# Sixteen-head attention: another order for VectorE, and a rounding copy handed from VectorE to GpSimd

## What is computed

```
mod = silu(c) @ W_mod + b_mod
sh, sc, g, ... = split(mod, 6)
h = layernorm(x) * (1 + sc) + sh
q, k, v = split(h @ W_qkv, 3)            # 16 heads of width 64
attn = softmax((q @ k.T) * 64 ** -0.5)   # per batch and head, 256 x 256
out = (attn @ v).reshape(B, T, 1024)
x = x + g * (out @ W_out + b_out)
```

## Time and profile before

| | before |
|---|---|
| time, median of 3 runs | 1752.8 us (1749.63 to 1753.22) |
| the profiled execution: span from the first to the last instruction | 1752.5 us |
| PE busy | 1626.4 us, 93% of the span |
| PEld busy | 1458.4 us, 83% |
| DVE busy | 1294.3 us, 74% |
| ACT busy | 1179.8 us, 67% |
| POOL busy | 1093.6 us, 62% |
| mean granted clock of TensorE, as a share of full speed | 0.978 |
| the chain that ended last, by engine | PE 64%, DVE 13%, issue 8%, POOL 6%, ACT 2% |

### The profile page before, as it was taken

One profiled execution on the slowest core, in us unless ns is written; L12 is line 12 of the kernel. 1 busy time (PEld: TensorE's weight loads), 2 busy tenths in 40 slices (PEclk: granted clock), 3 DMA queues, 4 the chain that ended last, 5 costly groups with the idle time before them and its releaser, 6 DMA issues.

```text
span 1752.5 us, 37390 instructions
## 1 busy us (share of the span) xinstructions
PE 1626.4 (93%) x13251; PEld 1458.4 (83%) x13251; DVE 1294.3 (74%) x2766; ACT 1179.8 (67%) x2896; POOL 1093.6 (62%) x1261
## 2 busy tenths in 40 slices
PE   4888998999999999999999789999999999989997
PEld 2557878888888888888888779999888889989997
DVE  3767768989898888888888745556788778864442
ACT  2545657777787777787777655556676667666663
POOL 1555667888888888888888622333555568842223
PEclk7999999999999999999999899999999999999999
DMA  8213310000000000000000011111122112221111
GB/s 306 61 49 86 88 42 11 11 10 11 11 7 6 11 10 11 11 11 11 10 11 10 1 32 30 31 31 32 48 57 58 45 27 46 47 52 37 37 49 48
DMA packets 110973, 65.93 MB, mean 38 GB/s; under 512 B 81530, under 2 KB 92788, under 8 KB 110788
## 3 DMA queue, kind: packets, MB, share of 16 engines
q1 hardware_dynamic: 110788, 63.54, 13.3%
HBM read 59.06 MB, written 4.46 MB: 36 GB/s over the span
## 4 chain that ended last, share of the span: by engine, by line
PE 64%; DVE 13%; issue 8%; POOL 6%; ACT 2%; DMA 0%; DVEq 0%; POOLq 0%; SPq 0%; ACTq 0%
PE bank L289 14%; PE bank L290 13%; PE bank L291 13%; POOL prob L1083 5%; PE s_banks L289 4%; PE bank L1105 4%; DVE ptlo L1120 4%; PE s_banks L290 4%; PE s_banks L291 4%; PE s_banks L1028 4%; PE bank L1131 3%; DVE of L1157 2%; PE bank L417 2%; DVE xn L376 2%; DVE oThi L1161 1%
## 5 line engine op out<-in xcount | busy, mean ns | idle before, releaser
L1083 POOL TENSOR_SCALAR prob<-prob,rinv 128x256 f32<-128x256 f32 x508 | 465.8, 935 | 117.0 <-DVE rinv L1064 117.0
L1055 ACT ACTIVATE prob<-s_banks,nmax 128x256 f32<-128x256 f32 x512 | 236.6, 475 | 17.4 <-DVE nmax L1045 17.4
L289 PE MATMUL bank<-WBhi,hl 128*128 128x256 f32 x768 | 219.0, 285 | 6.2 <-DVE upd L647 5.3
L290 PE MATMUL bank<-WBlo,hh 128*128 128x256 f32 x768 | 217.7, 283 | 0.0
L291 PE MATMUL bank<-WBhi,hh 128*128 128x256 f32 x768 | 215.5, 281 | 0.0
L1115 ACT ACTIVATE pthi<-bank 128x512 fp32r<-128x512 f32 x256 | 139.2, 596 | 100.9 <-PE bank L1105 98.8
L1045 DVE TENSOR_REDUCE nmax<-s_banks 128x4 f32<-128x1024 f32 x128 | 156.0, 1219 | 62.6 <-issue 61.9
L610 ACT ACTIVATE hh<-bank,vecs 128x512 fp32r<-128x512 f32 x120 | 82.9, 691 | 155.7 <-PE bank L291 155.7
L430 ACT ACTIVATE nThi<-bank,mod 128x256 fp32r<-128x256 f32 x192 | 110.5, 575 | 104.9 <-issue 75.7
L289 PE MATMUL bank<-aThi,WAlo 128*128 128x256 f32 x576 | 175.4, 304 | 0.6 <-DVE aTlo L438 0.2
L1120 DVE TENSOR_TENSOR ptlo<-bank,pthi 128x512 fp32r<-128x512 f32 x256 | 164.9, 686 | 4.0
(11 more groups left out here) (185 smaller groups left out, 5546.5 us busy)
## 6 DMA issues: line engine op xcount, KB each, us to landing
gates<-gate_scratch SPq DMA_DIRECT2D x96, 256.0 KB, 3.6
agate<-gate_scratch SPq DMA_DIRECT2D x32, 256.0 KB, 3.6
stage<-in_L_cond_W SPq DMA_DIRECT2D x64, 64.0 KB, 2.3
out<-x SPq DMA_DIRECT2D x16, 256.0 KB, 2.2
adaw<-in_L_cond_Wc SPq DMA_DIRECT2D x1, 3072.0 KB, 17.7
stage<-in_L_cond_W_qkv SPq DMA_DIRECT2D x8, 384.0 KB, 3.4
x<-in_x SPq DMA_DIRECT2D x1, 2560.0 KB, 16.6
stage<-in_L_cond_ff_w SPq DMA_DIRECT2D x32, 64.0 KB, 2.2
```

The source lines that it names most:

```text
L289: pe.matmul(dst, lhs[1], rhs[0], start=start, stop=False, skip_group_check=True)
L290: pe.matmul(dst, lhs[0], rhs[1], start=False, stop=False, skip_group_check=True)
L1055: last = act.activation(prob[h % 4][:, q, :], SB_[h % 2][:, q * SEQ:(q + 1) * SEQ], ACT.Exp, bias=of_head(nmax, h)[:, q:q + 1], accum_out= ...
L1083: last = pool.tensor_scalar(prob[h % 4][:, q, :], prob[h % 4][:, q, :], of_head(rinv, h)[:, q:q + 1], None, ALU.mult)
```

## The change

The copy of `of` to `oThi` leaves `o_add` and DVE and becomes the first instruction of `o_rest` on POOL, with the two waits that stood before it; POOL then waits for its own copy before it subtracts. In DVE's list, `o_add(n - 2)` comes ahead of `score_max(n + 2)`; statistics and normalisation come ahead of `proj_vector`; and 1/sum is made for pair n + 2 near the end of period n, ahead of the projections, where it was made for pair n + 1 at the start of period n. The first 1/sum of pair 1 moves to the end of `mh_start`.

```
-        def o_add(dve, pair, i):
+        def o_add(dve, pair):
             if pair:
                 dve.wait_ge(o_lo, pair)
...
                 dve.tensor_tensor(of[main, :], OB[main, cols], oc[main, :], ALU.add).then_inc(o_sum, 1)
-            dve.wait_ge(o_sum, 2 * pair + 2)
+
+        def o_rest(pool, pair, i):
+
+            pool.wait_ge(o_sum, 2 * pair + 2)
             if pair >= 2:
-                dve.wait_ge(out_mm, pair - 1)
-            dve.tensor_copy(oT[i][0][:, :], of[:, :]).then_inc(o_hi, 1)
-
-        def o_rest(pool, pair, i):
-
+                pool.wait_ge(out_mm, pair - 1)
+            pool.tensor_copy(oT[i][0][:, :], of[:, :]).then_inc(o_hi, 1)
             pool.wait_ge(o_hi, pair + 1)
             pool.tensor_tensor(oT[i][1][:, :], of[:, :], oT[i][0][:, :].bitcast(F32),
                                ALU.subtract).then_inc(o_lo, 1)
...
         def mh_vector(dve, b, j):
             n = PAIRS * b + j
-            if n + 1 < PERIODS:
-                prob_inverse(dve, n + 1)
             if j == 3 and b:
                 res_vector(dve, A, b - 1, YB, out_mm, PAIRS * b, b - 1)
+            if n >= 2:
+                o_add(dve, n - 2)
             if n + 2 < PERIODS:
                 score_max(dve, n + 2)
-            if n >= 2:
-                o_add(dve, n - 2, n % 2)
             for h in range(2):
                 pt_rest(dve, 2 * n + h)
             if j == NEXT - 1 and b + 1 < BATCH:
                 rows_vector(dve, b + 1)
-            for it in items(b, j):
-                proj_vector(dve, *it)
             if b + 1 < BATCH:
                 if j == 1:
                     ln_stats(dve, A, b + 1, 0)
                 if j == 2:
                     ln_norm(dve, A, b + 1, 0)
+            if n + 2 < PERIODS:
+                prob_inverse(dve, n + 2)
+            for it in items(b, j):
+                proj_vector(dve, *it)
             if j == NEXT:
                 weights_hi(dve, A + 1, b)
...
+            if name == "vector":
+                prob_inverse(eng, 1)
```

More of the change, by code:

```diff
@@ L1334, in mh_vector @@
             if n == PERIODS - 1:
-                o_add(dve, n - 1, (n - 1) % 2)
-                o_add(dve, n, n % 2)
+                o_add(dve, n - 1)
+                o_add(dve, n)
                 res_vector(dve, A, b, YB, out_mm, PAIRS * b + PAIRS, b)
```

## The result

The changed kernel takes 1768.87 us (median of 4 runs, 1766.43 to 1769.55); the kernel before, run beside it, 1751.89 us (4 runs, 1749.63 to 1753.22). The ratio is 1.01, with a 95% interval from 1.0088 to 1.0112: slower by 1.0%, where 0.7% was forecast. The profiled execution of the changed kernel has a span of 1767.8 us.

What follows compares the result with a forecast made beforehand. Four engines were nearly full together, so the order of handing work on was taken as the bound. Span 1752.5 plus 10.5 - 0.6 + 2 gives 1764.4, plus 0.3 gives 1764.7 us, 0.7% slower; range 1744 to 1779.

Steps and rivals of the forecast that it cites:

- The chain: Attention periods: exponentials, projection's high part, `o_read`, sums, maximum, exponentials close a ring; 5.47 us with one projection, 47.26 a batch.
- the two weight copies in j = 4: DVE, j = 4 to 5: they follow the projection's low part and add 0.47 us to a 5.67 us period.
- the steps: Period lengths summed over a batch: 47.26 us against 46.56, 0.70 more, so 10.5 us over 15 batches.
- not 0.6: First batch: 0.6 us less than the others, because it has no gated output in j = 3.
- The wait that was named: DVE: the maximum stands behind sums that wait for ACT's `o_read`; 0.88 us from `o_read` to the sums.
- my signs of being wrong: ACT's copy done before DVE is free for it, PE's busy share over 0.95, or POOL without idle time.
- my rival "faster": Shorter seams on ACT (0.48) and DVE (0.78) give 45.66 us a batch, 1740.7 us in all; chance 0.17.
- 0.5 and 0.1: POOL: rounding copy 0.5 us and its own wait before the subtraction 0.1; POOL busy 44.1 of 47.3 us a batch.
- the rival "same": DVE: only the hand-over from sums to maximum is shorter, 0.78 us; 46.46 a batch, 1752.7 in all; chance 0.20.
- the 0.64 between projection and `o_read`: ACT: `o_read` starts 0.64 us after the projection, the projection's whole 0.61 and 0.03, with no early start.
- 11.9 in all: Whole kernel: 10.5 us for 15 batches, less 0.6 for the first, plus 2 for the last (0 to 4 allowed).
- the 0.3 us between span and median: Whole kernel: the median lies 0.3 us above the profiled span, added to 1764.4 to give 1764.7 us.

Runs made afterwards that it cites:

- the kernel with the order alone: Kernel before, with only the sums, their rounding copy still on DVE, moved ahead of the maximum: 1831.26 us, ratio 1.045.
- the maximum in front: Changed kernel with the maximum of pair n + 2 again ahead of the sums of pair n - 2: 1715.29 us, ratio 0.9787 to the kernel before.
- The experiment without it: Changed kernel in which ACT copies a constant tile and the sums wait for PE's values only, output incomplete: 1750.91 us, ratio 0.9998.

## Why the prediction was right

**The chain.** It is the one predicted, and the periods, from maximum to maximum, agree link by link:

| period | predicted, us | measured, us |
|---|---|---|
| one projection (j = 7 to 0, 0 to 1) | 5.47 | 5.51, 5.50 |
| two projections (j = 1 to 2, 5 to 6, 6 to 7) | 5.95 | 5.99, 5.98, 5.98 |
| j = 2 to 3 | 6.38 | 6.42 |
| j = 3 to 4 | 6.42 | 6.43 |
| j = 4 to 5 | 5.67 | 5.50 |
| batch | 47.26 | 47.32; mean of 15: 47.39 |

One term was wrong by 0.2 us: the two weight copies in j = 4. I took 0.47 us of the list for them; here they take 0.27:

```profile
668.81 0.35 DVE L327 CAST WBhi<-stage 128x128 fp32r<-128x128 f32 x2
669.08 0.88 DVE L1157 TENSOR_TENSOR of<-bank,oc 64x256 f32<-64x256 f32 x2
```

The difference is not what follows the copies: in the kernel with the order alone 1/sum follows them, also after 0.27 us (702.91 and 703.18). It is what POOL does meanwhile. The first line below has the copies of the kernel before between 300 and 980 us (the least, median and longest time in ns), the second those of the changed kernel, and the third the subtraction on POOL beside which the first copy of the earlier trace rows lay:

```profile
L327 DVE CAST WBhi<-stage x28: 212/312/416, 334.8 to 940.5; 128x128 fp32r<-128x128 f32 x28
...
L327 DVE CAST WBhi<-stage x28: 216/219/224, 336.6 to 952.8; 128x128 fp32r<-128x128 f32 x28
...
660.73 0.73 POOL L1166 TENSOR_TENSOR oTlo<-of,oThi 128x256 fp32r<-128x256 f32 x1
```

Of the two copies in a batch of the kernel before, the one beside POOL's subtraction takes 0.41 us and the other 0.22. In the changed kernel the subtraction has ended (667.26 + 0.73) when the copies start at 668.81, and both take 0.22. With the rounding copy alone on POOL the subtraction covers nearly the whole of the first one (648.64 to 649.38), and it takes 0.79. The other seven periods came out 0.01 to 0.04 longer than predicted, which the short copies nearly made up for.

The 15 batches cost 12.5 us (710.89 - 698.34) where the steps gave 10.5. Three of them, the fourth, fifth and fifteenth, are 0.3 to 0.6 longer than the rest; with the maximum in front the same three are 0.15 to 0.4 longer, so much of it isn't the order's. Why, I did not follow up. The first batch gave 47.16, 0.2 less than the others and not 0.6.

**The wait that was named.** I put the new wait on ACT's copy, and in the five periods where I had it last it is the later of two ways, by 0.27 us or less. The experiment without it shows that the low parts of the projections, already ahead of the sums in DVE's list, would have closed nearly the same chain. Yet it decides the sign: without it a batch takes 46.57 us and the kernel 1750.91 us, no longer than before. So most of the 53.6 us that the order costs is the place of the sums, which the list of links held only for j = 2 to 4, while the 17 us by which the changed kernel is slower hang on the wait that I named. None of my signs of being wrong came: PE is busy 0.944 of the stretch, POOL stands idle for 11% of it, and ACT's copy is not done first in the periods of its chain. DVE's waits returned less at the sums (6.0 us) than before 1/sum (53.4), which I hadn't said. The price of the order is 3.1 us a batch against the same work with the maximum in front; my rival "faster" sought its gain in shorter seams and not there.

**POOL.** The copy takes 0.40 us with a gap of 0.08 behind it, against 0.5 and 0.1:

```profile
689.32 0.40 POOL L1164 CAST oThi<-of 128x256 fp32r<-128x256 f32 x1
689.80 0.73 POOL L1166 TENSOR_TENSOR oTlo<-of,oThi 128x256 fp32r<-128x256 f32 x1
691.02 3.64 POOL L1083 TENSOR_SCALAR prob<-prob,rinv 128x256 f32<-128x256 f32 x4 [0.49 <-DVE rinv L1064]
```

POOL is busy 0.8904 x 47.39 = 42.2 us a batch; I had 44.1. It still waits 47.1 us for 1/sum where I said hardly any. That wait is now its slack: it arrives early because the chain holds everything back, and with the maximum in front 14.3 us are left of it.

**The seams.** On DVE the maximum starts 0.91 us after the sums, where I took 0.88; the rival "same" with 0.78 falls. This is the place where the Trainium skill, "VectorE: DVE Perf Modes", section "Two Vector instructions with no wait between them", bore on the sum. The runs agree with its rule of the starting quadrant: the low halves, too, start only 1.26 us after the maximum's start where the sums stand in front of it, 683.21 - 681.95, and 1.14 us after it where the copy, which begins at partition 0, stands between sums and maximum (704.48 and 705.62 in the kernel with the order alone). I hadn't priced this second hold, 0.12 us on the low halves; it lies beside the exponentials' 1.26 us and not on the chain.

On ACT I had put the 0.64 between projection and `o_read` down to the change from 128 partitions to 64. The length held (0.63), the reason didn't. In the kernel whose sums don't wait for ACT, the copy has 64 partitions too and starts 0.48 us after the projection:

```profile
676.45 0.61 ACT L995 ACTIVATE qkhi<-bank 128x512 fp32r<-128x512 f32 x1
676.93 0.86 ACT L1149 ACTIVATE oc<-mod 64x256 f32<-64x256 f32 x2
```

There the first of the two copies reads a tile in SBUF from partition 0 on, where the kernel's own reads a bank of PSUM from partition 64 on. Which of the two makes the difference no run shows.

**The last batch.** POOL's wait in its j = 3, 5.46 us before, in the changed kernel:

```profile
996.04 0.24 POOL L366 TENSOR_SCALAR vareps<-meanvar 128x4 f32<-128x4 f32 x1 [7.45 <-DVE meanvar L359]
```

It grew by 2.0, and by the end of this attention the kernel is 14.1 us behind: 0.3 before the first counted maximum, 12.5 in the batches, 1.3 in the last; I allowed 11.9 in all.

**Behind the attention** I had put nothing. The one-head attention gives 1.1 us back (its last exponentials come 13.0 us later than before). Then the first twelve products of the next phase run at the lower clock, 0.50 or 1.2 GHz, where they had 1.00 or 2.4 GHz. The clock in two 2 us stretches, of the kernel before

```profile
1556.00:1558.00 2.00, 1.79 (x8) 1.47 (x9) 1.23 (x7) 0.00 (x0) 1.78 (x4) 1.00 0.84 269
```

and of the changed kernel, the same products:

```profile
1570.00:1572.00 2.00, 2.00 (x6) 1.52 (x6) 0.00 (x0) 0.00 (x0) 1.85 (x3) 0.50 0.86 290
```

These twelve start over 4.86 us (1569.58 to 1574.44) where they started over 2.67 (1556.21 to 1558.88), which costs 2.2 us and makes the 15.3 us between the two spans. PE had been idle 2.49 us just before them, against 1.50; ahead of that idle time it had run at 0.50 in both kernels, and in the kernel before the clock had risen again by 1556. It doesn't go with the order of the calls: in the traces of the experiments the twelve start over 4.86 us in two kernels (the copy alone, and the sums that don't wait for ACT), over 4.1 to 4.2 in three, and over 2.67 in three, among them the changed kernel with one more copy on POOL. So these 2.2 us aren't a price of the change that its other executions must show, and whether they do isn't known; the medians differ by 17.0 us. I also read the 0.3 us between span and median as what lies around the span. In each of the kernels here the profiled execution's own time is 1.7 to 1.9 us above its span (1769.55 and 1767.8 for the changed one), so that of before probably lay some 1.5 us above its median, an estimate from 1752.5 + 1.8 against 1752.8. By that step the forecast can be off by about 1.5 us.

## What to carry to other kernels

Write each engine's list as a ring, and ask of every instruction that you move ahead of another what it waits for: if that stems from the result of the one behind it, you have closed a chain through the period, and its links, read from the trace before, add up to the new period, here within 0.04 us in seven of eight periods. Work that sits in such a ring costs in full, work beside it little (0.5 of 2.3 us a batch on POOL), so the parts of a change can't be priced one by one and added. The length of a link can also change with what another engine does beside it, as that of the weight copies did. Here the two other parts both pay, and with the maximum left in front they give 1715.3 us, 2.1% under the kernel before and 3.0% under the changed one, with PE at 99% of the stretch.

## What was not expected of the hardware

A GpSimd copy of 128x256 takes 399 ns and its subtraction of two such tiles 737, while its multiplication by one value per partition takes 927, more than either. The groups of POOL in the changed kernel between 300 and 980 us (busy us, mean ns, then idle before):

```profile
L1083 POOL TENSOR_SCALAR prob<-prob,rinv 128x256 f32<-128x256 f32 x460 | 419.2, 927 | 47.6 <-DVE rinv L1064 47.1
L1166 POOL TENSOR_TENSOR oTlo<-of,oThi 128x256 fp32r<-128x256 f32 x116 | 85.5, 737 | 10.0
L1164 POOL CAST oThi<-of 128x256 fp32r<-128x256 f32 x116 | 46.3, 399 | 0.0
```

I had placed the copy between a fill and the subtraction, at 0.5 us for the doubt. The multiplication is POOL's main load, with 419 us of its busy time in this stretch (its 460 instructions overlap a little), so the form of that one instruction should decide how near POOL is to its bound; no run here changes it.

DVE's copies and normalisations depend on what POOL runs beside them. A normalisation of 128x256 takes 0.40 us with POOL idle, 0.53 to 0.58 beside POOL's multiplication, and 0.75 us or more beside a two-input instruction that covers most of it, 1.36 in the case above.
